# A block of attention, LoRA-expert FFN and state-space mixer: masks of the FFN's second half later, the last block split by slot, LoRA-down in token quarters

## What is computed

```python
x = x + attention(layernorm(x))
x = x + ffn(layernorm(x))        # first FFN
x = x + mixer(layernorm(x))
x = x + ffn(layernorm(x))        # second FFN, same weights

def ffn(x):                      # 8 experts, 2 chosen, LoRA rank 16, hidden width 704
    topw, sel = top_k(x @ gate_w.T, 2)
    topw = softmax(topw, axis=1)             # over the tokens
    for e in range(8):
        c = sum(where(sel == e, topw, 0))
        up   = x @ w_up.T   + 2 * (x @ up_A[e].T   @ up_B[e].T)
        gate = x @ w_gate.T + 2 * (x @ gate_A[e].T @ gate_B[e].T)
        ch = c * silu(up) * gate
        mixed += ch
        lora_down += 2 * (ch @ down_A[e].T @ down_B[e].T)
    return mixed @ w_down.T + lora_down
```

## Time and profile before

| | us |
|---|---|
| runs of the kernel before | 568.29, 570.72, 571.48 |
| median | 570.72 |
| the profiled execution, its own time | 568.28 |
| its span, first to last instruction | 566.5 |
| TensorE busy | 525.1 (93%) |
| VectorE busy | 405.4 (72%) |
| ScalarE busy | 307.6 (54%) |
| GpSimd busy | 127.2 (22%) |

### The profile page before, as it was taken

How to read it: one execution, slowest core, us unless ns; L and a number is a source line. 1 busy time by engine, 2 the same in 40 slices (tenths; PEclk the granted TensorE clock), 3 DMA queues, 4 the chain that set the end, 5 groups by cost and what they waited for, 6 DMA issues and landing times.

```text
span 566.5 us, 9078 instructions
## 1 busy us (share of the span) xinstructions
PE 525.1 (93%) x3047; PEld 441.1 (78%) x3049; DVE 405.4 (72%) x895; ACT 307.6 (54%) x758; POOL 127.2 (22%) x272
## 2 busy tenths in 40 slices
PE   6998899999999888799999999999899889999994
PEld 4777799998999877577887887757777668788883
DVE  6534565666566878799877888957876868877684
ACT  3655778688677742454342455888752244333341
POOL 2322324244243210000000004667542000000000
PEclk9999999999999999999999999999999999999998
DMA  7320100000004003000030000000000000000101
GB/s 264 109 75 1 38 2 2 2 1 1 2 2 144 2 1 135 1 1 1 0 131 0 1 2 0 1 1 1 2 0 2 1 0 2 0 2 0 38 1 38
DMA packets 5790, 14.25 MB, mean 25 GB/s; under 512 B 624, under 2 KB 2928, under 8 KB 5744
## 3 DMA queue, kind: packets, MB, share of 16 engines
q1 hardware_dynamic: 5744, 13.66, 6.9%
HBM read 12.61 MB, written 1.05 MB: 24 GB/s over the span
## 4 chain that ended last, share of the span: by engine, by line
PE 65%; DVE 19%; ACT 7%; issue 6%; POOL 1%; DMA 1%; DVEq 0%; ACTq 0%; POOLq 0%
PE psum L167 53%; PE psum L468 2%; DVE f_t L1203 2%; DVE f_um L1213 2%; DVE oT_hl L697 1%; PE psum L500 1%; PE psum L235 1%; DVE ln_stats L207 1%; DVE x_resid L704 1%; ACT qT L566 1%; PE psum L997 1%; ACT pT_hl L598 1%; DVE xT_hl L249 1%; ACT f_sil L1110 1%; PE psum L1611 1%
## 5 line engine op out<-in xcount | busy, mean ns | idle before, releaser
L167 PE MATMUL psum<-xT_hl,ffn_w_hl 128*128 128x512 f32 x312 | 78.1, 397 | 7.3 <-DVE f_t L1203 7.3
L167 PE MATMUL psum<-f_um,ffn_w_hl 128*128 128x512 f32 x288 | 72.1, 398 | 1.2 <-DVE f_um L1213 1.2
L167 PEld LDWEIGHTS psum<-xT_hl,ffn_w_hl 128*128 128x128 f32 x312 | 56.3, 188 | 19.6 <-issue 8.7
L167 PEld LDWEIGHTS psum<-f_um,ffn_w_hl 128*128 128x128 f32 x288 | 53.5, 188 | 14.3 <-DVE f_um L1213 2.1
L1203 DVE TENSOR_TENSOR f_t<-psum,f_sil 128x512 f32<-128x512 f32 (+1 forms) x48 | 33.2, 691 | 32.8 <-ACT f_sil L1110 32.2
L1110 ACT ACTIVATE f_sil<-psum 128x512 f32<-128x512 f32 (+1 forms) x48 | 28.3, 597 | 51.8 <-PE psum L167 51.8
L167 PE MATMUL psum<-wo_hl,oT_hl 128*128 128x256 f32 x384 | 50.9, 282 | 4.1 <-DVE oT_hl L697 4.0
L691 DVE TENSOR_TENSOR pT_hl<-psum,pT_hl 126x360 fp32r<-126x360 f32 (+1 forms) x44 | 23.6, 537 | 42.9 <-ACT pT_hl L598 42.9
L167 PE MATMUL psum<-xT_hl,wq_hl 128*128 128x512 f32 x192 | 52.3, 407 | 1.9 <-ACT qT L566 1.9
L167 PEld LDWEIGHTS psum<-wo_hl,oT_hl 128*128 128x128 f32 x384 | 47.7, 188 | 7.5 <-DVE oT_hl L697 5.8
L1131 ACT ACTIVATE f_ch_hl<-f_ch 128x512 fp32r<-128x512 f32 x48 | 30.1, 630 | 41.4 <-DVE f_ch L1260 41.3
(11 more groups left out here) (238 smaller groups left out, 1128.6 us busy)
## 6 DMA issues: line engine op xcount, KB each, us to landing
w_raw<-in_wq SPq DMA_DIRECT2D x4, 512.0 KB, 3.9
w_raw<-in_wo SPq DMA_DIRECT2D x4, 512.0 KB, 3.3
ffn_w_raw<-in_ffn SPq DMA_DIRECT2D x3, 576.0 KB, 6.3
ffn_w_raw_far<-in_ffn SPq DMA_DIRECT2D x3, 576.0 KB, 5.1
ssd_w_raw<-in_ssd SPq DMA_DIRECT2D x3, 512.0 KB, 5.4
x_resid<-in_x SPq DMA_DIRECT2D x2, 512.0 KB, 4.6
out_x<-x_resid SPq DMA_DIRECT2D x4, 256.0 KB, 2.3
w_raw<-in_wk SPq DMA_DIRECT2D x1, 512.0 KB, 6.6
```

The costliest lines, as they stand in the source:

```text
L167: i = e.matmul(dst, lhs(a), rhs(b), start=start and n == 0, stop=stop and n == len(TERMS) - 1, **kw)
```

## The change

It has these parts, all in the FFN:

1. Front: `base_x(0)` is split, its gate half goes behind the transposes of half 1. `ln["norm"](1)` goes ahead of `top_index(0)` on VectorE. The logit copy of half 1 goes from VectorE to ScalarE. `masks` is called slot by slot, both mask copies are made by ScalarE (`mask_out`), and VectorE only subtracts them (`mask_diff`). In ScalarE's list `silu(0, 1)` goes ahead of `weights_out(0)`.
2. Half 1's masks: `top_index(1)` goes to iteration 2 of VectorE, `one_hot(1)` to iteration 3, `masks(1, ...)` to iteration 5 on TensorE and into bank 3, with `mask_out` on ScalarE. `masked(1, ...)` goes to iterations 5 (0 and 1 ahead of slot 0, 2 behind it, 3 at the end with `mask_diff`) and 6 (4 and 5 behind slot 0, 6 and 7 at the end). In iteration 6 TensorE does `second(5)` ahead of `base_lora(6)`.
3. Weight splits in iterations 1 to 4, one piece each.
4. Iteration 8: `gated(7, 1)` goes ahead of `add(0)`; the statistics of the next layer norm go to iteration 9, `w_lo_out` of the mixer from iteration 9 to 10.
5. Last block: ScalarE and VectorE split slot 0 ahead of slot 1's silu and gate product; `down` waits slot by slot.
6. LoRA-down: `dd` and `d_hl` are made in two halves of 256 columns, `lora_down` waits and signals for two tiles of 128 tokens at a time, and each addition waits for its own two tiles.

```diff
                 else:
                     need(e, "mk0", 1)
-                    need(e, "mk1", 2)
+                    need(e, "mk1", 1)
...
-            def masks(e, h):
-
-                need(e, "ulo", 2 * h + 2)
-                need(e, "hot", 2 * h + 2)
-                for s in range(SLOTS):
-                    for t in range(HT):
-                        m = e.matmul(bank(4 + s)[:, t * P:(t + 1) * P], hot[:, s, HT * h + t, :], identb,
-                                     start=True, stop=True)
-                    m.then_inc(FS["mk"], 1)
+            MASK_BANK = ((4, 5), (3, 3))
+            LORA_COLS = (slice(0, HALF // 2), slice(HALF // 2, HALF))
+            MASK_STEP = HB - 2
+
+            def masks(e, h, s):
+
+                need(e, "hot", 2 * h + s + 1)
+                if h == 0:
+                    need(e, "ulo", 2)
+                elif s == 0:
+                    need(e, "t1", MASK_STEP)
+                else:
+                    need(e, "mk0", 2)
+                for t in range(HT):
+                    m = e.matmul(bank(MASK_BANK[h][s])[:, t * P:(t + 1) * P], hot[:, s, HT * h + t, :], identb,
+                                 start=True, stop=True)
+                m.then_inc(FS["mk"], 1)
...
                 ln["tr"](e, 1)
+                base_x(e, 0, (1,))
                 base_x(e, 1, (0,))
                 logits(e, 1)
-                masks(e, 0)
+                for s in range(SLOTS):
+                    masks(e, 0, s)
...
-                    need(e, "chl", 2 * (i + 1))
                     for s in range(SLOTS):
+                        need(e, "chl", 2 * i + s + 1)
                         m = three(e, bank(6 + s), lambda w: blk(w, b, FB_DA, ER),
                                   lambda w: ch_hl[:, i % 2, s, w, :], b == 0, b == HB - 1)
-                    if b == HB - 1:
-                        m.then_inc(FS["da"], 1)
+                        if b == HB - 1:
+                            m.then_inc(FS["da"], 1)
...
-                    need(e, "dl", h + 1)
                     for t in range(HT):
+                        if t % 2 == 0:
+                            need(e, "dl", 2 * h + t // 2 + 1)
...
-                    m.then_inc(FS["y"], 1)
+                        if t % 2:
+                            m.then_inc(FS["y"], 1)
 
                 for i in range(N + 2):
                     if 2 <= i < N:
                         base_x(e, i)
                         if i == 2:
-                            masks(e, 1)
                             weigh(1)
+                        if i == MASK_STEP + 1:
+                            masks(e, 1, 0)
+                        if i == MASK_STEP + 2:
+                            second(i - 1)
                         base_lora(e, i)
                     if i == N:
                         early(phase, "tr0", e)
-                    if 2 <= i <= N:
+                    if 2 <= i <= N and i != MASK_STEP + 2:
                         second(i - 1)
+                    if i == MASK_STEP + 1:
+                        masks(e, 1, 1)
...
+                def mask_out(h, s):
+                    need(e, "mk", 2 * h + s + 1)
+                    e.activation(mT[:, s, half(h)], bank(MASK_BANK[h][s]), ACT.Copy).then_inc(FS[("mk0", "mk1")[s]], 1)
...
                 ln["hi"](e, 1)
+                need(e, "lg", 2)
+                e.activation(lgT[:, :], bank(6)[0:EXPERTS, :], ACT.Copy).then_inc(FS["lgt"], 1)
                 before["free"](e)
-                mask0(0)
+                for s in range(SLOTS):
+                    mask_out(0, s)
...
+                silu(0, 1)
                 weights_out(0)
-                silu(0, 1)
...
                 for i in range(N + 1):
                     if i == HB + 2:
                         lora_hi(0)
+                    if i == MASK_STEP + 1:
+                        mask_out(1, 0)
                     if 1 <= i < N:
                         silu(i, 0)
                     if i == 1:
                         split(4)
-                        mask0(1)
+                    if i == N:
+                        hi_slot(i - 1, 0)
                     if i >= 2:
                         silu(i - 1, 1)
+                    if i == MASK_STEP + 1:
+                        mask_out(1, 1)
...
+                def mask_diff(h):
 
                     need(e, "mk0", h + 1)
-                    need(e, "mk", 2 * h + 2)
-                    e.tensor_copy(mT[:, 1, half(h)], bank(5)).then_inc(FS["mk1"], 1)
-                    e.tensor_tensor(mT[:, 2, half(h)], bank(5), mT[:, 0, half(h)], ALU.subtract).then_inc(FS["mk1"], 1)
+                    need(e, "mk1", h + 1)
+                    e.tensor_tensor(mT[:, 2, half(h)], mT[:, 1, half(h)], mT[:, 0, half(h)],
+                                    ALU.subtract).then_inc(FS["mk2"], 1)
...
                 top(e, 0)
+                ln["norm"](e, 1)
                 top_index(e, 0)
-                ln["norm"](e, 1)
...
                 one_hot(0)
-                logits_copy(e, 1)
-                mask1(0)
                 top(e, 1)
...
                 masked(0, 2, 3)
+                mask_diff(0)
...
-                masked(0, 4, 5, 6)
+                masked(0, 4, 5, 6, 7)
                 gated(0, 0)
-                masked(0, 7)
                 split(3)
-                top_index(e, 1)
                 gated(0, 1)
...
                 def lora_mask(h):
-                    need(e, "da", h + 1)
                     if h:
-                        need(e, "dl", h)
+                        need(e, "dl", 2 * h)
                     for s in range(SLOTS):
+                        need(e, "da", 2 * h + s + 1)
...
-                    e.tensor_tensor(dd[:, 2, :], dd[:, 0, :], dd[:, 1, :], ALU.add).then_inc(FS["dd"], 1)
-                    need(e, "dh", h + 1)
-                    e.tensor_tensor(d_hl[:, LO, :], dd[:, 2, :], f32(d_hl[:, HI, :]), ALU.subtract).then_inc(FS["dl"], 1)
+                    for cols in LORA_COLS:
+                        e.tensor_tensor(dd[:, 2, cols], dd[:, 0, cols], dd[:, 1, cols], ALU.add).then_inc(FS["dd"], 1)
+                    for n, cols in enumerate(LORA_COLS):
+                        need(e, "dh", 2 * h + n + 1)
+                        if h:
+                            need(e, "y", n + 1)
+                        e.tensor_tensor(d_hl[:, LO, cols], dd[:, 2, cols], f32(d_hl[:, HI, cols]),
+                                        ALU.subtract).then_inc(FS["dl"], 1)
...
-                        one_hot(1)
+                    if i == MASK_STEP + 1:
+                        masked(1, 0, 1)
                     if i < N and i != 1:
                         slot(i, 0)
-                    if 3 <= i <= 5:
-                        masked(1, *range(3 * (i - 3), min(3 * (i - 2), 8)))
-                    if i == HB + 2:
-                        add(0)
+                    if i == MASK_STEP + 1:
+                        masked(1, 2)
+                    if i == MASK_STEP + 2:
+                        masked(1, 4, 5)
+                    if i == HB + 3:
                         early(phase, "stats", e, *range(HT))
                         early(phase, "veps0", e)
                     if i == HB + 4:
                         early(phase, "norm0", e)
+                    if i == HB + 2:
+                        gated(i - 1, 1)
+                        add(0)
+                    if i == N:
+                        lo_slot(i - 1, 0)
                     if i >= 1:
                         if i == 1:
                             gated(1, 0)
                         slot(i - 1, 1)
-                        if i == 1:
-                            mask1(1)
...
+                    if i == MASK_STEP + 1:
+                        masked(1, 3)
+                        mask_diff(1)
+                    if i == MASK_STEP + 2:
+                        masked(1, 6, 7)
+                    if 1 <= i <= 4:
+                        split(i + 3)
+                    if i == MASK_STEP - 2:
+                        top_index(e, 1)
+                    if i == MASK_STEP - 1:
+                        one_hot(1)
```

More of the change, by code:

```diff
@@ L1083, in a_hi @@
                                      scale=ALPHA).then_inc(FS["uhi"], 1)
-                def mask0(h):
-                    need(e, "mk", 2 * h + 1)
-                    e.activation(mT[:, 0, half(h)], bank(4), ACT.Copy).then_inc(FS["mk0"], 1)
+                def mask_out(h, s):
+                    need(e, "mk", 2 * h + s + 1)
+                    e.activation(mT[:, s, half(h)], bank(MASK_BANK[h][s]), ACT.Copy).then_inc(FS[("mk0", "mk1")[s]], 1)
                 if first:
@@ L1119, in weights_out, with hi_slot @@
                         e.activation(wb[:, s, half(h)], bank(wb_bank(h, s)), ACT.Copy).then_inc(FS["wbc"], 1)
+                silu(0, 1)
                 weights_out(0)
-                silu(0, 1)
+                def hi_slot(i, s):
+                    if i >= 2:
+                        need(e, "d", i - 1)
```

(42 more changed lines are left out.)

17 lines of the change are left out of this document (8 added, 9 removed).

## The result

The changed kernel takes 555.06 us at the median of four runs (554.99 to 557.08), the kernel before 569.50 (568.15 to 571.48, four runs). The ratio is 0.9752 with a 95% interval of 0.9711 to 0.9794. The profiled execution of the changed kernel is the slowest of its four, 557.08, with a span of 555.3 against 566.5.

A forecast was written before the change was run, and what follows sets the result against it. TensorE, busy 93% of the span, was taken as the bound, so only its idle time could be won. First FFN 4.9, second 3.3 and tail 3.3 summed to 11.5 us: 570.72 to 559.2, stated as 559, range 554.5 to 563.5.

The forecast's parts named there:

- tail: End of second FFN: mask products 1.5 us earlier, halves of dd 0.9, overlapped additions 0.8; 3.3 together.
- Step (a): FFN front: index search behind second layer-norm half, six matmuls behind transposes; 0.3 us in first FFN, 0.8 in second.
- (b): FFN front: logit and mask copies go to ScalarE; stall of 0.78 us goes, transposes 0.25 earlier; 1.3 with (a)'s 0.3.
- Step (d): FFN front: silu(0,1) swapped ahead of router-weight copies on ScalarE; whole 2.16 us stall at base_x(2) goes, sum 3.3.
- Step (c): Up to second(0): VectorE gets mask_diff, 0.60 us, of which 0.35 fills an idle wait; gain falls from 1.3 to 1.1.
- Step (e): Iterations 0 to 2: VectorE loses one-hot rows and mask conversions; 0.9 us, mask matmuls away 0.5, sum 4.7 at base_x(3).
- The stall at base_x(7): Iteration 6: new TensorE stall waiting for gated(5,1), with only down(4) behind base_lora(6); 1.4 us lost.
- the upper bound: Tail: 3.9 us instead of 3.3 if lora_down also keeps its clock.
- R4: Rival, chance 0.02: slower, the stall in iteration 6 lowers TensorE's clock; 576 us with 8.3 us of such work per FFN.
- R1: Rival, chance 0.04: gain mainly lost again in iterations 5 to 9 as VectorE falls behind; 567.8 us.
- R3: Rival, chance 0.18: smaller gain, silu's swap brings only half and the tail its lower bound of 1.5 us; 563 us.
- R2: Rival, chance 0.15: 3 us more gain from lora_down's clock, cheap mask_diff and overlapped losses of iterations 8 and 9; 556.

The follow-up runs named there:

- e10: Changed kernel with base_x(0) whole ahead of the transposes and the index search ahead of the layer norm again; 558.11 us median.
- e1: Changed kernel with the two copies of router weights ahead of silu(0,1) on ScalarE again; 563.51 us median.
- e2: Kernel before the change with only silu(0,1) put ahead of the two copies of router weights on ScalarE; 565.89 us median.
- e4: Changed kernel with top_index(1) and one_hot(1) put back into iteration 0 on VectorE; 557.71 us median.
- e3: Changed kernel with half 1's masked operands 4 to 7 moved ahead of slot(6,0) in iteration 6 on VectorE; 552.94 us median.
- e11: Changed kernel with second(5) back behind base_lora(6) in iteration 6 on TensorE; 553.88 us median.
- e6: Changed kernel with the last block's slot 0 split back behind slot 1's product; 557.34 us median.
- e12: Changed kernel with down waiting for both slots' low parts before its first matmul and signalling da once; 556.77 us median.
- e5: Changed kernel with LoRA-down's dd and d_hl made in one piece of 512 columns again; 558.29 us median.
- e8: Changed kernel with masked operands 4 to 7 ahead of slot(6,0) and iteration 9's layer-norm statistics behind lo_parts; 554.22 us median.

## Why the prediction was right, point by point

Gains by position, against the attention's last stall in the first FFN (213.10 and 213.01) and against the transposition of half 0's logits in the second (438.55 and 434.49):

| step | forecast | measured |
|---|---|---|
| second(0), first FFN | 1.1 | 1.23 |
| base_x(2) | 3.3 | 3.50 |
| base_x(3) | 4.7 | 5.06 |
| base_x(10) | 4.3 | 4.93 |
| first matmuls behind half 1's layer norm in the mixer | 4.9 | 5.45 |
| base_x(3), second FFN | 4.2 | 4.58 |
| base_x(9), second FFN | 3.3 | 3.82 |
| tail | 3.3 | 3.24 |
| sum | 11.5 | 12.5 |

**The front.** Step (a) holds in both FFNs (e10). Steps (a) and (b) together bring the first transposition of the softmax values 1.22 earlier against the attention's last stall (it starts at 228.18 before, at 226.87 after), forecast was 1.3; (b) was not undone by itself. Step (d), the swap, is the largest term and right in cause and size (e1, e2). Step (c) left 0.1 more than forecast. mask_diff took 0.42 us where a 32-bit product takes 0.69, and it stands among VectorE operations that follow each other without a pause up to the product that second(0) waits for, so the 0.27 were there to be won; where the rest of them went was not looked into. Here the Trainium skill was right: "VectorE: DVE Perf Modes", section "The perf-mode tier table (the rule you actually need)", has a bf16 `tensor_tensor` in SBUF at twice the rate, the 0.27 us less that stood beside the sum; the trace has 0.69 - 0.42 = 0.27. Step (e) is right in the first FFN (e4).

**Iterations.** The stall at base_x(7), forecast as 1.4, measures 1.36 + 0.16, the wait of second(6) 0.33 (matmuls of 3.29 instead of 2.96) against 0.3, and the one behind the statistics 0.43 + 0.16 against 0.6. Down(6) lost 0.34 + 0.16 for the additions, where 0.7 was forecast. From base_x(3) to base_x(10) the change costs 0.13 (62.05 us before, 62.18 after), where the steps had 0.4. In pieces: iterations 3 to 5 gained 1.03 (forecast 0.7), 6 and 7 cost 1.86 (1.7), 8 gained 1.22 (1.2), 9 cost 0.52 (0.6). The moves of iterations 3 to 5 and 8 and of the weight splits were not undone one by one; for them the positions speak. That the stall in iteration 6 is a matter of order is shown by e3 and e11, not only argued.

**The tail.** The sum is right, but partly by luck: its parts are not, and they add up to 3.2 where 3.3 was written. From second(11) to the mask products 1.40 us are won (7.74 before, 6.34 after; forecast 1.5). But of this the early split of slot 0, on which I had built the step, gives nothing (e6). 1.07 comes from waiting and signalling by slot in down (e12). The rest is a pause of 0.45 before mix(11) in the kernel before (552.63 to 553.08, also in e2's trace) which is 0.1 in the changed one, and 0.1 in both at every other slot sum that stands right behind its product. It is 0.1 in e6 as well, so the early split is not what removes it; I did not find out what it is. From there to lora_down 0.75 (e5 shows it; 0.9 forecast). From lora_down to the end of the additions 1.09, of which 0.49 is lora_down's 1.64 against 2.13: at full clock, which I had put into the upper bound only; the overlap of additions and matmuls is then 0.6, not 0.8.

**Forecast against medians.** By the two profiled executions the gain is 11.2, by position 12.5: the changed kernel's profiled execution lost 1.5 in a clock dip at the mixer's end, which its fastest runs (554.99, mean clocks of 0.999 and 1.00) by their clocks don't have. The medians differ by 14.4. So of the 3.9 by which the forecast is too high, 1.0 is in the terms. 2.4 came in at its last step, which put the gain under the median of 570.72 and not under the profiled 568.28, as if the changed kernel would slow down from its undisturbed execution to its median as the one before did; three of its four executions did not. The last 0.5 is not accounted for. That the median is inside the range is thus in part luck: a count by position from 568.28 gives 555.8. Of the 1.9 between 12.5 and 14.4, 1.2 lie in the executions of the kernel before, whose median is 569.50 and whose profiled one took 568.28. In eleven of them beside e5 to e8 the fastest took 568.35 at a mean clock of 0.995, those at 0.992 about 570.5 to 571.0, those at 0.986 573.5. The changed kernel's four have 0.996 to 1.00. That the front stalls bring such dips on is what e1 suggests (rival R4's mechanism, working for the change instead of against it): it was seen in one profiled execution, and nothing shows how often it happens. Of four stalls of 2 us in the fronts (two in the kernel before, two in e1) one was followed by a dip.

**Rivals.** R1 and R3 are refuted by the traces: VectorE had the room, the swap brought its whole 2.2 in each FFN, and the tail brought 3.24 and not its lower bound. R2, the larger gain, was right by 1 us of its 3 by position: lora_down kept its clock, mask_diff was cheaper, and iterations 3 to 5 gained more. R4 did not happen at base_x(7): after the 1.36 us stall the clock stayed at 1.00 in every profiled execution.

## What to carry to other kernels

When an in-order engine stands idle before the bounding one's stall, look at the entries right ahead of the late one in its queue: the largest term here was two copies that nobody needed yet, ahead of a silu that everybody waited for, and the change itself put in another such order that cost 3 us. Write the chain out once from a stall that the trace shows (start to start, with its latencies) and reuse it with one operation more or less; it gave each stall that the prediction named for the iterations within 0.2 us. Compare variants between the same two instructions of their traces; medians carry the drift of stages that were not touched.

## What the runs showed of the hardware

TensorE's granted clock falls to the lower level (1.2 GHz) for a few microseconds in some executions, at two places while the kernel runs on, and at a third at its end. One is behind a stall of 2 us at base_x(2) (e1, above). The second is the end of the mixer, behind a stall of 1.03 us that all kernels have there. In the changed kernel it is at

```profile
425.00:430.00 5.00, 3.97 (x25) 3.63 (x24) 4.03 (x11) 1.62 (x4) 0.55 (x1) 0.80 0.00 0
430.00:435.00 5.00, 5.00 (x22) 3.81 (x22) 1.95 (x7) 1.00 (x2) 1.56 (x2) 0.86 0.00 0
```

and in e8 it is absent, with the same stall of 1.03 ahead:

```profile
425.00:430.00 5.00, 5.00 (x32) 4.48 (x32) 3.92 (x12) 0.00 (x0) 1.10 (x2) 1.00 0.00 0
```

The third is lora_down(1): behind 2.18 us of idle TensorE its twelve matmuls took 2.13 in the kernel before and 2.53 in e2, there at the lower level for most of it (the row is of e2):

```profile
558.00:560.00 2.00, 1.97 (x10) 1.67 (x8) 0.00 (x0) 0.00 (x0) 0.00 (x0) 0.50 0.00 0
```

Behind 1.86 us (e5), 1.50 (e12) and 1.11 they took 1.64, at full clock. One dip at the first two places costs 1.5 to 1.6 us of matmul time (1.51 between the mixer's last stall and the transposed logits; 4.58 - 3.02 in e1). Eight of the fourteen profiled executions have one at one of the first two places or at both. So executions of the same program lie some 2 us apart, and where a dip follows a stall, the two together cost more than the stall's length. That the stall brings the dip on is suggested by where the dips stand and not shown; what decides whether one comes stays open: 2.00 us at the same place in the kernel before was not followed by one.
